# Softmax denominators of the late queries from one sum made by GpSimd, in a fused conv-gate, attention and expert layer

## The reference

```python
q, k, v = (x @ w.T).reshape(B, S, H, D).transpose(0, 2, 1, 3)      # for w_q, w_k, w_v; S = 256, H = 16, D = 32
scores = SOFTCAP * jnp.tanh(jnp.einsum('bhsd,bhtd->bhst', q, k) * SCALE / SOFTCAP)
scores = jnp.where((j <= i) & (i - j < WINDOW), scores, -1e+30)    # causal; WINDOW = 256
probs = jax.nn.softmax(scores, axis=-1)
attn = jnp.einsum('bhst,bhtd->bhsd', probs, v)
```

## Time and profile before

| | us |
|---|---|
| runs shown | 779.08, 779.13, 778.22 (median 779.08) |
| profiled execution | 779.08 |
| its span | 777.3 |
| PE busy | 651.7 (84%) |
| DVE busy | 418.4 (54%) |
| POOL busy | 281.0 (36%) |
| ACT busy | 270.4 (35%) |

### The profile page before, as it was taken

How to read it: one execution, slowest core, us unless ns; L and a number is a source line. 1 busy time by engine, 2 the same in 40 slices (tenths; PEclk the granted TensorE clock), 3 DMA queues, 4 the chain that set the end, 5 groups by cost and what they waited for, 6 DMA issues and landing times.

```text
span 777.3 us, 13639 instructions
## 1 busy us (share of the span) xinstructions
PE 651.7 (84%) x4859; PEld 526.3 (68%) x4860; DVE 418.4 (54%) x1022; ACT 270.4 (35%) x462; POOL 281.0 (36%) x324
## 2 busy tenths in 40 slices
PE   0001279999999999999989999999799999999991
PEld 0000178887878787878768989999666667666670
DVE  7898635465646564647364798322434444444441
ACT  7340006463636363636362312434312221122210
POOL 1780002241323232323141111774544554445531
PEclk9999999999999999999999999999899999999997
DMA  8440000010101010102022643342646555665543
GB/s 298 140 158 0 0 1 1 2 56 2 54 0 54 0 54 0 54 0 83 1 83 84 248 139 113 110 135 69 247 91 107 98 97 104 108 100 97 103 65 40
DMA packets 24787, 62.08 MB, mean 80 GB/s; under 512 B 3057, under 2 KB 7153, under 8 KB 23729
## 3 DMA queue, kind: packets, MB, share of 16 engines
q1 hardware_dynamic: 15344, 41.16, 15.4%
q0 software_dynamic: 8736, 20.45, 14.9%
q10 hardware_dynamic: 672, 0.03, 0.1%
HBM read 38.56 MB, written 23.07 MB: 79 GB/s over the span
## 4 chain that ended last, share of the span: by engine, by line
PE 52%; DMA 24%; DVE 14%; issue 5%; ACT 1%; POOL 1%; DVEq 1%; SPq 0%; POOLq 0%
DMA out_tokens<-yo,dest 24%; PE PS L1373 21%; PE scores L1373 12%; PE PS L1468 5%; PE scores L1602 5%; PE scores L1454 3%; PE PS L1423 2%; DVE v L873 2%; DVE col L884 1%; DVE rden L1049 1%; PE PS L1412 1%; DMA T<-in_x 1%; DVE col L888 1%; DVE qT L813 1%; DVE qT L814 1%
## 5 line engine op out<-in xcount | busy, mean ns | idle before, releaser
L1373 PE MATMUL scores<-xb,sw 128*128 128x256 f32 x768 | 97.7, 283 | 0.0
L1373 PEld LDWEIGHTS scores<-xb,sw 128*128 128x128 f32 x768 | 95.1, 191 | 2.1 <-issue 0.4
L571 POOL DMA_INDIRECT out_tokens<-yo,dest x39 | 61.7, 1583 | 93.1 <-DMA out_tokens<-yo,dest 91.0
L1373 PE MATMUL PS<-xt_h,w_h 128*128 128x256 f32 x256 | 76.1, 297 | 3.6 <-issue 2.1
L491 POOL TENSOR_SCALAR_AFFINE_SELECT probs<-probs 128x256 f32<-128x256 f32 x128 | 51.5, 430 | 66.6 <-ACT probs L649 66.5
L1683 PE MATMUL scores<-wd_sb,ehT 128*128 x156 | 73.5, 593 | 1.0 <-DVE ehT L1333 1.0
L1373 PE MATMUL PS<-xt_l,w_h 128*128 128x256 f32 x256 | 73.3, 286 | 0.0
L1373 PE MATMUL PS<-xt_h,w_l 128*128 128x256 f32 x256 | 73.2, 286 | 0.0
L764 ACT ACTIVATE es<-scores 128x256 f32<-128x256 f32 x39 | 15.0, 384 | 164.3 <-PE scores L1373 160.2
L1373 PE MATMUL scores<-wgu_h,xgT_h 128*128 x156 | 65.7, 421 | 4.4 <-DVE xgT_l L1337 4.4
L1049 DVE RECIPROCAL rden<-PS 128x256 f32<-128x256 f32 x32 | 56.1, 1754 | 23.9 <-PE PS L1468 23.9
(11 more groups left out here) (255 smaller groups left out, 1366.7 us busy)
## 6 DMA issues: line engine op xcount, KB each, us to landing
wgu_l<-in_wgu SPq DMA_DIRECT2D x8, 1024.0 KB, 6.7
T<-in_x SPq DMA_DIRECT2D x8, 512.0 KB, 8.0
probs<-in_wqkvo SPq DMA_DIRECT2D x8, 512.0 KB, 4.1
x_rows<-x SPq DMA_DIRECT2D x8, 512.0 KB, 2.8
x_cols<-x2T SPq DMA_DIRECT2D x8, 512.0 KB, 2.7
xc<-x_cols SPq DMA_DIRECT2D x8, 512.0 KB, 3.6
out_tokens<-T SPq DMA_DIRECT2D x8, 512.0 KB, 7.5
wd_sb<-in_wd SPq DMA_DIRECT2D x8, 512.0 KB, 6.9
```

The lines of the kernel that those rows point to most:

```text
L571: pool.indirect_dma_start(out[:, :], bass.IndirectOffsetOnAxis(dest[:, t:t + 1], 0), yo[:, t % 3, :], None, compute_op=ALU.add).then_inc(y ...
L1373: ins = pe.matmul(out, lhs(k, a), rhs(k, b), start=m == 0, stop=m == len(products) - 1)
```

## The change

After its two affine selects, `mask` now also waits for them on a new semaphore, `masked_late`, and adds, with one tensor_tensor on GpSimd, the masked probabilities of the late queries against the early keys to those against the late keys. The result goes to a new tile `late_sum` (two heads of 128 columns, four buffers), and this instruction signals `mask_done`. The product with v is as it was. The product with ones takes the early queries' 128 columns from `probs` and the late queries' 128 columns from `late_sum`, in place of 256 columns and then 128 more that are added to them. A few small tiles change their addresses to make room.

```diff
-        PROBS, SMALL, BATCH = 4 * 2 * 384, 1840, CB * S
+        PROBS, SMALL, BATCH = 4 * 2 * 384, 1864, CB * S
...
+        scope = area("late_sums", PROBS)
+        late_sum = sb("late_sum", [P, 4, 2, P], fp32, scope)
...
-                ins.then_inc(mask_done, 1)
+                ins.then_inc(masked_late, 1)
+                pool.wait_ge(masked_late, 8 * b + p + 1)
+                t = probs[:, p % 4, :].rearrange("p (h q) -> p h q", h=2)
+                pool.tensor_tensor(late_sum[:, p % 4, :, :], t[:, :, P:S], t[:, :, S:S + P],
+                                   ALU.add).then_inc(mask_done, 1)
...
-                for off, lhs in ((0, lambda h, tt: v[:, tt, h * D:(h + 1) * D]), (S, lambda h, tt: ones[:, 0:D])):
-                    for tt in range(TT):
-                        for j in range(HC):
-                            h = HC * c + j
-                            pr = probs[:, (h // 2) % 4, 384 * (h % 2):384 * (h % 2 + 1)]
-                            ins = pe.matmul(od_bank[j * D:(j + 1) * D, off + tt * P:off + S], lhs(h, tt),
-                                            pr[:, 0:S] if tt == 0 else pr[:, S:S + P], start=tt == 0, stop=tt == TT - 1,
-                                            skip_group_check=True)
+                for tt in range(TT):
+                    for j in range(HC):
+                        h = HC * c + j
+                        pr = probs[:, (h // 2) % 4, 384 * (h % 2):384 * (h % 2 + 1)]
+                        pe.matmul(od_bank[j * D:(j + 1) * D, tt * P:S], v[:, tt, h * D:(h + 1) * D],
+                                  pr[:, 0:S] if tt == 0 else pr[:, S:S + P], start=tt == 0, stop=tt == TT - 1,
+                                  skip_group_check=True)
+                for tt in range(TT):
+                    for j in range(HC):
+                        h = HC * c + j
+                        early = probs[:, (h // 2) % 4, 384 * (h % 2):384 * (h % 2) + P]
+                        ins = pe.matmul(od_bank[j * D:(j + 1) * D, S + tt * P:S + (tt + 1) * P], ones[:, 0:D],
+                                        late_sum[:, (h // 2) % 4, h % 2, :] if tt else early, start=True, stop=True,
+                                        skip_group_check=True)
                 ins.then_inc(pv_done, 1)
```

More of the change, by code:

```diff
@@ L156, in layer_kernel @@
         probs = sb("probs", [P, 4, 2 * 384], fp32, scope)
+        row = sb("row", [1, 8, B * UP], fp32, scope)
+        g_avg = sb("g_avg", [P, P], fp32, scope)
+        g_med = sb("g_med", [B * UP, B * UP], fp32, scope)
+        col = sb("col", [B * UP, 24], fp32, scope)
+        sb("below_rden", [P, 8], fp32, scope)
         rden = sb("rden", [P, S], fp32, scope)
@@ L171, in layer_kernel @@
         coefB = sb("coefB", [P, B * CB], fp32, scope)
[L172 to L175, removed]
+        scope.close()
+        scope = area("late_sums", PROBS)
+        late_sum = sb("late_sum", [P, 4, 2, P], fp32, scope)
         scope.close()
@@ L306, in layer_kernel @@
             sem("scores_full"), sem("tanh_done"), sem("exp_done"), sem("mask_done"))
+        masked_late = sem("masked_late")
         pv_done, att_ready, att_h_done, att_l_done = (
```

## The result

The changed kernel takes 789.61 us (median of 4 runs, 789.21 to 790.59), the kernel before 779.11 (median of 4): ratio 1.0136, 95% interval 1.0115 to 1.0158. It is slower, as forecast, but by 10.5 us where 3.2 were forecast, and outside the range.

What follows compares the result with a forecast made beforehand. PE was taken to bound the kernel through attention, then a chain of 39 transfers. Batch 0 0.0, five mid steps +1.7, batch 6 +0.5 and batch 7 +1.0 made +3.2 on 779.08: 782.3 us, range 777.8 to 785.5.

Steps and rivals of the forecast that it cites:

- What bounds, and that nothing behind attention gives it back: PE bounds up to about 571 us, then 39 chained transfers; a change in attention's end moves the kernel's end.
- The delay at values 1: Mid step: masks 2 and 3 with their sums let PE start values 1 0.77 us later, at 243.99 against 243.22.
- The no-contention rival: Sums run at 0.74 and mask 3 at 0.77 beside L1019; values 1 +0.29, total 778.5 us; chance 0.22.
- The saving of 0.21 a chunk: Ones products on PE: narrower columns save 0.21 us a chunk, 6.8 us over 32 chunks; values 0's is waited away.
- PE has no gap there but one: Attention, batch 3: PE's only gap is the 1.23 us wait for DVE's `att` before values 3.
- L996 keeps its 1.47: a sum beside it replaces selects that slowed its last instruction: Four DVE instructions before chunk 2's reciprocal stay at 1.47 us; bounds -0.09 to +0.27 us.
- my own signs of being wrong: Steps of 38.0 or less, no `late_sum` wait before values 1, L996 over 1.6 us, or first scatter not moving with attention.
- The clock in the mid steps: No half-clock term in the five mid steps (+1.7 us), though the wait before values 3 was to grow by 0.2.
- Batches 0 and 6: Batch 0: gains eaten at values 3, 0.0; batch 6: values 3 bound by its mask, +0.46 us.
- Batch 7: Late masks: +0.62 us at full clock, +1.42 if a half-clock stretch ends at the same moment; middle +1.0 taken.
- The blocked rival: POOL stands still while L1019 runs: values 1 +1.44, L996 adds 0.27, a step +1.28, total 787.9 us; chance 0.12.
- my rates: POOL beside DVE's L1019: `att_l` works at a rate of 0.4, selects at 0.69, a slowdown and not a full stop.

Runs made afterwards that it cites:

- chunks 0 to 2: Kernel after with the sums and the short ones product in chunks 0, 1 and 2 only, chunk 3 as before: 781.81 us, 1.004.
- delay on the short product: Kernel before with ones product of 256 columns per head, no sums, plus one bn_stats on DVE before chunk 2's reciprocal in mid steps: 782.31 us, 1.0055.
- with both: Kernel before with L996 behind chunk 2's reciprocal and the second norm's power behind mask 3: 769.91 us; with sums and short product in chunk 2 alone: 769.41.
- power alone moved: Kernel after with the second norm's power on GpSimd moved behind mask 3 and its sum, L1006 left in place: 784.41 us, 1.0074.
- short product alone: Kernel before with the 256-column ones product and no sums, late denominators leaving out the early keys: 773.49 us, 0.9918.
- sums alone: Kernel after with the old ones product of 384 columns, sums made and waited for but not read: 788.48 us, 1.010.
- delay alone: Kernel before with one more bn_stats on DVE before chunk 2's reciprocal in the five mid steps, no sums: 782.3 us, 1.0042.

## Why the prediction was wrong

What bounds the kernel was right, what the sums cost on the way was not: 3.2 us forecast, 10.5 measured.

- **What bounds, and that nothing behind attention gives it back:** right. +10.56 us at the last values, +10.1 at the end.
- **The delay at values 1:** forecast 0.77, measured 0.70. Its parts were not as I had them. I let the first sum be slowed to 1.10 us beside the norm and mask 3 to 0.89; they took 0.74 and 1.14. The sum was undisturbed, the selects paid. The no-contention rival, with 0.29, was wrong.
- **The saving of 0.21 a chunk:** right, 0.22. That values 0 loses it was right, for the wrong cause: `xt_l` takes it before the masks can. "PE has no gap there but one" was wrong: there is this second one, 0.37 us long.
- **"L996 keeps its 1.47: a sum beside it replaces selects that slowed its last instruction":** this step failed. They take 1.98, and over 1.6 was one of my own signs of being wrong. I had bounded the cost at 0.27, from the 500 ns that one of them takes beside selects; it was 0.51, since nowhere in the trace of before does a POOL tensor_tensor lie beside these four. It stands on the path, in front of a reciprocal for which PE already waited. A mid step at full clock is so 0.82 longer, not 0.34: 4.1 us for five, where 1.7 were forecast. The experiment with chunks 0 to 2 shows it: without these sums the four are back at their old time and the step at 38.5.
- **The clock in the mid steps:** this failed too; it was put at nothing without a reason. I asked what the clock does in batch 7, where a half-clock stretch was to be seen, and not what a longer wait before values 3 does to it in the steps that had none. I had even forecast that wait to grow by 0.2. Three stretches of 1.5 us are 4.4 us, the largest term. The delay on the short product shows that a longer idle brings them without any sum; which of the steps fall stays open.
- **Batches 0 and 6:** forecast 0.0 and 0.46, measured 0.0 and 0.3.
- **Batch 7:** forecast +1.0, between 0.6 and 1.4; measured +1.9 in this execution. My upper end let the half-clock stretch end at its old moment, with PE at work for 1.6 us of it. It came later instead, as values 1 did, and PE worked 3.1 us in it (the window from 401.80). By my own sum, as an estimate, that makes 0.6 + 1.5 = 2.1. How long the stretch lasts differs among the profiled kernels: 3.4 to 13.7 us, and two had none.
- **The blocked rival** (787.9, chance 0.12) came nearest, but not by its parts: it had 1.44 us at values 1 and 0.27 at L996, and no clock.

The rule of the Trainium skill that I had weighed ("SBUF — State Buffer", Who interferes with whom) was nearer at L1006 than my rates. In batch 3 one of the four took 0.83 us where alone it takes 0.41, with a sum of 0.91 beside it, and two took 0.49. That is a wait of about half a sum. But it was not a full stop for each: the 0.74 of the sum that L1029 began beside shows no loss on either side. I had also read the rule one way only: it gives the ports to whichever instruction is issued first, DVE's or GpSimd's, and the blocked rival, which I tied to it, let DVE alone have them.

## What to carry to other kernels

Work moved to a free engine is paid where it meets its neighbours, not in its own busy time. Ask of each place which instruction of another engine lies beside it and whether that one is on the path; 16 of 64 sums did most of the damage, and as many in the one chunk with slack gained. Where PE already waits, first ask what it waits behind: moving four DVE instructions past a reciprocal was worth 6 us, the best place for the sums 0.2 us a step (by the medians 3.0 us with one move, 0.5 with both). The change and that move must be judged apart: with the move in both kernels, sums in every chunk still cost 6.7 us. And an idle gap on PE that grows by tenths of a microsecond may cost more than those tenths, in clock: here 1.5 us each time.

## What the runs showed of the hardware

- In the profiled executions, of 15 mid steps with an idle of 1.94 to 2.03 us before values 3 (kernel after, delay on the short product, power alone moved), 8 had half clock behind it. Of 25 with 1.22 to 1.82 us (before, short product alone, chunks 0 to 2, sums alone, delay alone), none had. All 15 are of kernels with the short product in chunk 3.
- A stretch of half clock behind values 3 with PE busy throughout made the step 1.5 us longer.
- In batch 7, where PE has several idle gaps, 12 of the 14 profiled kernels had a stretch of half clock of 3.4 to 13.7 us.
- DVE's tensor_scalars of 128x256, alone 400 to 410 ns, took up to 834 (and 871 in the kernel before with them moved) beside a POOL tensor_tensor, and 486 to 500 beside POOL's selects. A POOL pair of selects took 1.14 us beside L1029, where alone it takes 0.77.
